# Reordering the rounds of attention on one core: maxima, scores, scores, maxima, and a unit's two projections side by side

## The reference, cut to what matters

```python
qk = x @ W_qk                        # 128 -> 2 * 16 * 64; values are the keys
q, k = jnp.split(qk, 2, axis=-1)     # 16 heads of 64
scores = einsum('bhid,bhjd->bhij', q * BETA, k)
scores = jnp.where(causal_mask, mask_value, scores)
attn = jax.nn.softmax(scores, axis=-1)
out = einsum('bhij,bhjd->bhid', attn, k)
return out.transpose(0, 2, 1, 3).reshape(b, n, 1024) @ W_out
```

## Time and profile before

| | before |
|---|---|
| median of 3 runs | 784.04 us (783.72 to 785.32) |
| the profiled execution | 783.28 us, of which 781.5 us from first to last instruction |
| busy: TensorE / VectorE / ScalarE / GpSimd | 729.7 / 458.5 / 375.6 / 424.4 us |
| mean granted clock of TensorE | 0.989 |

### The profile page before, as it was taken

One profiled execution on the slowest core, in us unless ns is written; L12 is line 12 of the kernel. 1 busy time (PEld: TensorE's weight loads), 2 busy tenths in 40 slices (PEclk: granted clock), 3 DMA queues, 4 the chain that ended last, 5 costly groups with the idle time before them and its releaser, 6 DMA issues. The chain is left out here.

```text
span 781.5 us, 14916 instructions
## 1 busy us (share of the span) xinstructions
PE 729.7 (93%) x5653; PEld 495.2 (63%) x5653; DVE 458.5 (59%) x1216; ACT 375.6 (48%) x476; POOL 424.4 (54%) x311
## 2 busy tenths in 40 slices
PE   2779999999999999999999998999989999789998
PEld 1456556555655655655655554887878875668887
DVE  5766665675676675576567540257565547766542
ACT  2355546545555545554654544235644534565421
POOL 4346865775684685676677567015455331344443
PEclk9699999999999999999999999999999999999999
DMA  2000010010010100101001001733222000033222
GB/s 67 7 7 20 19 32 16 22 28 15 22 28 16 25 23 22 25 18 29 15 15 28 16 23 33 177 81 97 76 89 95 29 1 0 3 118 108 91 95 81
DMA packets 41275, 33.47 MB, mean 43 GB/s; under 512 B 14002, under 2 KB 32756, under 8 KB 41204
## 3 DMA queue, kind: packets, MB, share of 16 engines
q1 hardware_dynamic: 41204, 32.52, 14.5%
HBM read 23.32 MB, written 1.31 MB: 32 GB/s over the span
## 5 line engine op out<-in xcount | busy, mean ns | idle before, releaser
L407 POOL TENSOR_TENSOR all_x<-all_x,at_probs 128x1024 f32<-128x1024 f32 (+3 forms) x128 | 215.3, 1682 | 31.8 <-ACT at_probs L487 17.1
L487 ACT ACTIVATE at_probs<-at_ring 128x1024 f32<-128x1024 f32 x144 | 147.5, 1026 | 123.0 <-PE at_ring L662 115.9
L532 DVE CUSTOM_DVE_ANT_0 at_ring<-at_ring,at_after_query 128x128 f32<-128x128 f32 (+3 forms) x256 | 119.5, 520 | 66.3 <-PE at_ring L627 66.3
L680 PE MATMUL at_out<-at_probs,at_k_nat 128*64 128x512 f32 (+3 forms) x768 | 140.3, 494 | 1.1 <-DVE a_attn_t L558 0.9
L407 POOL TENSOR_TENSOR all_x<-at_probs 128x768 f32<-128x768 f32 (+1 forms) x32 | 66.9, 2092 | 126.6 <-ACT at_probs L487 126.4
L1134 POOL TENSOR_TENSOR m_prod<-m_gate,m_wb 128x512 f32<-128x512 f32 x64 | 82.9, 1304 | 96.0 <-ACT m_gate L989 86.1
L680 PEld LDWEIGHTS at_out<-at_probs,at_k_nat 128*64 128x64 f32 x768 | 49.2, 136 | 70.0 <-issue 66.1
L528 DVE TENSOR_REDUCE at_half_max<-at_ring 128x2 f32<-128x1024 f32 x64 | 75.4, 1221 | 11.8 <-PE at_ring L627 11.8
L1043 DVE TENSOR_TENSOR m_hid<-m_prod,m_u 128x512 f32<-128x512 f32 x64 | 43.3, 685 | 66.5 <-POOL m_prod L1134 66.3
L653 PE MATMUL at_ring<-at_qh,at_kh 64*128 64x512 f32 (+3 forms) x384 | 73.8, 380 | 6.1 <-DVE at_m_rows L546 2.6
L909 PEld LDWEIGHTS m_acc<-rest_wd,m_hid 128*128 128x128 f32 x576 | 74.7, 191 | 6.0
(11 more groups left out here) (244 smaller groups left out, 1256.6 us busy)
## 6 DMA issues: line engine op xcount, KB each, us to landing
m_wb<-m_wt_far SPq DMA_DIRECT2D x128, 128.0 KB, 2.9
at_inv<-at_inv_q SPq DMA_DIRECT2D x240, 32.0 KB, 1.8
all_x<-in_L_attn_a_x SPq DMA_DIRECT2D x8, 256.0 KB, 3.7
at_w_raw<-in_L_attn_a_W_qk SPq DMA_DIRECT2D x8, 128.0 KB, 2.8
out<-all_x SPq DMA_DIRECT2D x4, 256.0 KB, 3.9
a_room<-in_L_attn_a_W_out SPq DMA_DIRECT2D x1, 512.0 KB, 4.1
m_raw_wg<-in_L_ffn_experts_wg SPq DMA_DIRECT2D x1, 512.0 KB, 4.2
m_raw_wu<-in_L_ffn_experts_wu SPq DMA_DIRECT2D x1, 512.0 KB, 4.1
```

Source lines behind the costliest of these rows:

```text
L407: return pool.tensor_tensor(sums[:, :, a * P:b * P], left, right, ALU.add)
L487: act.activation(probs[:, :, slot * BANK:(slot + 1) * BANK], pair("S", unit, slot)[:, :, :], ACT.Exp, scale=BETA).then_inc(exp_done, 1)
L532: last = dve.tensor_tensor_reduce(out=sums_ps, in0=sums_ps, in1=after_query[:, BANK - w:BANK], scale=1.0, scalar=MASKED, op0=ALU.add, op1= ...
L680: last = pe.matmul(out_ps[rows(l), o:o + (b - a) * P], k_nat[g % 3][:, j, rows(l)], probs[:, l, at:at + (b - a) * P], start=(j == 0), stop ...
```

## The change

- `ROUNDS` gets a new order. Each round has maxima at both ends and scores between them: M S M in round 0, M S S M in the others. M0 and M1 move from round 1 to round 0.
- The projection Q of a unit moves from round 0 of the unit before to the end of round 4 one unit earlier, directly behind K; for unit 1 it moves in front of the loop. Its copy on ScalarE and its subtraction on VectorE move with it.
- `keys_low` moves on VectorE from the end of round 4 to the end of round 0 of the next unit. Before the loop, queries_low(1) now stands ahead of keys_low(1).
- A new function `mask` issues the mask's matmuls for all diagonal tiles of a slot before its scores. They open the accumulation in the slot's banks, and the scores of such a slot add to them. For slots 1 and 7 the mask is issued ahead of the maxima that stand before the slot.

```diff
-ROUNDS = [[("S", 0)], [("S", 1), ("M", 0), ("S", 2), ("M", 1)], [("S", 3), ("M", 2), ("S", 4), ("M", 3), ("M", 4)],
-          [("S", 5), ("M", 5), ("S", 6), ("M", 6), ("M", 7)], [("M", 8), ("S", 7), ("M", 9), ("S", 8)]]
+ROUNDS = [[("M", 0), ("S", 0), ("M", 1)], [("mask", 1), ("M", 2), ("S", 1), ("S", 2), ("M", 3)],
+          [("M", 4), ("S", 3), ("S", 4), ("M", 5)], [("M", 6), ("S", 5), ("S", 6), ("M", 7)],
+          [("mask", 7), ("M", 8), ("S", 7), ("S", 8), ("M", 9)]]
+DIAGONAL = [slot for slot in range(NSLOT) if any(a == j for j, a, _ in SLOTS[slot])]
...
 # scalar queue
                 keys_high(1)
+                queries_high(1)
...
-                        if r == 0 and more:
-                            queries_high(unit + 1)
                         if r == NBURST - 1 and unit + 2 < UNITS:
                             keys_high(unit + 2)
+                            queries_high(unit + 2)
...
 # vector queue
                 join_maxima(0)
+                queries_low(1)
                 keys_low(dve, 1)
...
                             if unit:
                                 scale_out(unit - 1, 0)
-                            if more:
-                                queries_low(unit + 1)
                         for what, m in row:
                             if what == "M" and more:
                                 maxima(unit + 1, m)
+                        if r == 0 and unit and more:
+                            keys_low(dve, unit + 1)
...
                             if more:
                                 max_rows(unit + 1)
                             if unit + 2 < UNITS:
-                                keys_low(dve, unit + 2)
+                                queries_low(unit + 2)
...
 # tensor queue
+                def mask(unit, slot):
+                    if slot == 0:
+                        pe.wait_ge(rows_done, unit + 1)
+                    pair_free(pe, "S", unit, slot)
+                    diagonal = [(at_slot(slot, seg) - slot * BANK) for seg, (j, a, _) in enumerate(SLOTS[slot]) if a == j]
+                    for o in diagonal:
+                        for h in range(2):
+                            for l in range(2):
+                                pe.matmul(pair("S", unit, slot)[:, l, o:o + P], mask2[rows(l), h, :], eye2[rows(l), h, :],
+                                          start=(o == 0 and h == 0), stop=False, skip_group_check=True)
...
-                            pe.matmul(to[l], kh[u][rows(l), keys], qh[u][rows(l), q], start=True, stop=False)
+                            pe.matmul(to[l], kh[u][rows(l), keys], qh[u][rows(l), q], start=first, stop=False,
+                                      skip_group_check=True)
...
-                        for h in range(2 if a == j else 0):
-                            for l in range(2):
-                                pe.matmul(to[l][:, 0:P], mask2[rows(l), h, :], eye2[rows(l), h, :], start=False, stop=False)
...
                 project(1, "K")
+                project(1, "Q")
...
+                            if what == "mask":
+                                mask(unit, n)
+                            elif what == "S":
+                                if n in DIAGONAL and ("mask", n) not in row:
+                                    mask(unit, n)
                                 scores(unit, n)
...
-                        if r == 0 and more:
-                            project(unit + 1, "Q")
                         if r == NBURST - 1 and unit + 2 < UNITS:
                             project(unit + 2, "K")
+                            project(unit + 2, "Q")
```

More of the change, by code:

```diff
@@ L224, in ring_uses @@
 def ring_uses():
-    uses = [("K", 0, 0), ("Q", 0, 0), ("T", 0, 0)] + [("M", 0, m) for m in range(NMAX)] + [("K", 1, 0)]
+    uses = [("K", 0, 0), ("Q", 0, 0), ("T", 0, 0)] + [("M", 0, m) for m in range(NMAX)] + [("K", 1, 0), ("Q", 1, 0)]
     for unit in range(UNITS):
@@ L231, in ring_uses @@
                 uses.append(("T", unit + 1, 0))
-            uses += [(what, unit if what == "S" else unit + 1, n) for what, n in row if what == "S" or more]
-            if r == 0 and more:
-                uses.append(("Q", unit + 1, 0))
+            uses += [(what, unit if what == "S" else unit + 1, n) for what, n in row if what == "S" or what == "M" and more]
             if r == NBURST - 1 and unit + 2 < UNITS:
-                uses.append(("K", unit + 2, 0))
+                uses += [("K", unit + 2, 0), ("Q", unit + 2, 0)]
     return uses
@@ L638, in turn_max @@
                           .then_inc(rows_ps_ready, 1)
+                def mask(unit, slot):
[8 more added lines that the diff above has]
+                                          start=(o == 0 and h == 0), stop=False, skip_group_check=True)
                 def scores(unit, slot):
-                    u, out = unit % 2, pair("S", unit, slot)
+                    u, out, first = unit % 2, pair("S", unit, slot), slot not in DIAGONAL
                     if slot == 0:
@@ L652, in scores @@
                         for l in range(2):
-                            pe.matmul(to[l], kh[u][rows(l), keys], qh[u][rows(l), q], start=True, stop=False)
+                            pe.matmul(to[l], kh[u][rows(l), keys], qh[u][rows(l), q], start=first, stop=False,
+                                      skip_group_check=True)
                         for l in range(2):
-                            pe.matmul(to[l], kh[u][rows(l), keys], ql[u][rows(l), q], start=False, stop=False)
+                            pe.matmul(to[l], kh[u][rows(l), keys], ql[u][rows(l), q], start=False, stop=False,
+                                      skip_group_check=True)
                         for l in range(2):
-                            pe.matmul(to[l], kl[u][rows(l), keys], qh[u][rows(l), q], start=False, stop=False)
-                        for h in range(2 if a == j else 0):
-                            for l in range(2):
-                                pe.matmul(to[l][:, 0:P], mask2[rows(l), h, :], eye2[rows(l), h, :], start=False, stop=False)
+                            pe.matmul(to[l], kl[u][rows(l), keys], qh[u][rows(l), q], start=False, stop=False,
+                                      skip_group_check=True)
                         for l in range(2):
-                            last = pe.matmul(to[l], ones_r[rows(l), :], m_rows[u][rows(l), q], start=False, stop=True)
+                            last = pe.matmul(to[l], ones_r[rows(l), :], m_rows[u][rows(l), q], start=False, stop=True,
+                                             skip_group_check=True)
                             if seg + 1 == len(SLOTS[slot]):
@@ L729, in _ @@
                         for what, n in row:
-                            if what == "S":
+                            if what == "mask":
[3 more added lines that the diff above has]
+                                    mask(unit, n)
                                 scores(unit, n)
```

## The result

The changed kernel takes 762.39 us (median of 4 runs, 761.02 to 762.94) against 784.68 us before (4 runs, 783.72 to 786.04): ratio 0.971, 95% interval 0.969 to 0.974. The forecast was 763.6, inside 758 to 771.

The account below looks back on a forecast made before the run. TensorE was taken to set attention's length, with gain only from its standstills. Thirteen periods (-21.1), the start (+1.7) and the last full unit (-1.0) sum to -20.4 us, giving 763.6, range 758 to 771 (8 in 10).

Parts of the forecast that it names:

- Order of the rounds: Reordered maxima and scores in the rounds: all five TensorE stalls at the bank ring go, -1.36 us a period, at least -0.89.
- five standstills: TensorE waits at the ring of three bank pairs: 0.30, 0.17, 0.30, 0.16 and 0.43 us, 1.36 a period.
- Q beside K: Projection Q directly behind K at the end of round 4: 1.73 us instead of 2.02, -0.29 a period, bounds 0 to -0.39.
- Masks first: Masks issued before a slot's scores: same matmuls, taken as 0 a period, bounds 0 and -0.24.
- The chain of Q: Next unit's Q copy, max_rows, queries_low before the first mask of S0 at t = 3.33 after turn_max: cost 0, bounds 0 and +0.5.
- keys_low: Moved on VectorE behind round 0's maxima: cost 0; +2.6 us in all if it took its longest, 2.42 us.
- Period: One turn_max to the next in mid-attention: -1.62 us, from 28.21 to 26.6; thirteen of them give -21.1.
- The start: Queue before the loop delays unit 0's first scores: second turn_max at 66.0 instead of 64.31, +1.7 us, bounds +0.5 and +2.8.
- The last full unit: Unit without projections behind its last maxima, so turn_max waits: 25.6 us instead of 26.61, -1.0, bounds 0 and -2.8.
- more: Rival: doubled masks pay once (-3.1 us) and the start loses little (-1.2): 759.3 us, chance 0.12.
- part given back in round 0: Rival: S0 and M1 stall behind the copies in round 0, 0.5 us a period, +6.5: 770.1 us, chance 0.15.
- The slower one: Rival: K copy, Q copy and queries_low delay S0's mask, 2.15 us a period, +28: 791 us, chance 0.04.

Follow-up runs that it names:

- e1: Kernel before with only the projection Q moved beside K, old round order and masks: period 28.00 us, 781.03 us, ratio 0.996.
- e2: Changed kernel with the mask's matmuls back inside each segment, ahead of its last two matmuls: period 26.83 us, 768.69 us, ratio 0.979 to the kernel before.
- e3: Changed kernel with the last scores of round 4 (S8) again behind the last maxima (M9): period 26.91 us, 767.16 us, ratio 0.977 to the kernel before.
- e10: Changed kernel with masks of slots 1 and 7 directly ahead of their scores, behind the maxima, still grouped: period 26.71 us, 766.82 us, ratio 0.977.
- e5: Changed kernel with keys_low back at the end of round 4 on VectorE, in front of queries_low: period 27.30 us, 774.63 us, ratio 0.989.
- after_again: The changed kernel itself, unaltered, run again: period 26.48 us, 762.30 us, ratio 0.971 to the kernel before.
- e6: Changed kernel with M9 ahead of S8 in the last full unit (14) alone: period 26.48 us, 760.00 us, ratio 0.969 to the kernel before.
- e4: Changed kernel with the old order of maxima and scores in rounds 1 to 3: period 27.38 us, 776.77 us, ratio 0.989 to the kernel before.
- e7: Changed kernel with turn_max(0) between unit 1's K and Q, max_rows(0) ahead of queries_low(1), keys_low(1) behind unit 0's M1 maxima: 759.74 us, ratio 0.970.
- e9: e8 plus S0 ahead of M0 in round 0 and keys_low behind M2's maxima: period 26.48 us, 757.35 us, ratio 0.965 to the kernel before.
- e8: Changed kernel with the edits of e6 and e7 together: period 26.48 us, 758.61 us, ratio 0.967 to the kernel before.

## Why the prediction was right

The time was within 1.2 us and the mechanism the one given, but several terms were off and cancelled in part.

- *Order of the rounds*: -1.36 forecast, -1.18 measured (e1 to e2). All five standstills went, and e3 shows the one at S8 to be worth 0.43 as read. What came back is mostly at M1: not only the wait of 0.03 to 0.05 that I had put down, but 0.10 more on the step that had waited. I called the gap between M3 and S4 the shortest, at 2.27 us; it is not. Between M4 and M5, and M6 and M7, lie only two slots of 0.93, and there the slack is 0.40.
- *Q beside K*: -0.29 forecast, -0.20 measured (e1). I gave S0's last step its 0.23 back, but it still stands before 128-row work in e1 and stays at 0.42.
- *Masks first*: 0 forecast with a bound of 0.24; 0.35 measured. This bound failed. I had said that there is no pair of adjacent masks; there is, in the three slots with two diagonal tiles, whose second mask now stands behind the first, and I had put it down as worth 0.08 each at most. What I missed is the place: behind outputs the bf16 masks take up the 0.10 of the change of rows (e10, 0.23 of the 0.35).
- *The chain of Q* and *keys_low*: cost 0, as forecast. The mask starts at t = 3.36 (forecast 3.33), queries_low is done at 2.86 (2.95), and keys_low is 1.22 in all units. e5 shows what the lost slack costs: 0.82.
- *Period*: 26.6 forecast, 26.48 measured. The parts are -1.18, -0.20 and -0.35, -1.73 in all, where I had -1.36, -0.29 and 0.03, -1.62: the masks gave more than the two others lost, and that the sum comes so near is in part luck.
- *The start*: the second turn_max at 66.0 forecast, 66.12 measured (66.50 in after_again), by luck. Q ended earlier, because the clock rose within the projections (steps of 0.23 from 38.12 on), and S0 started at 44.02, not 44.7; but the wait of 3.04 in front of it was followed by the low clock until past 51 us, which I hadn't in the sum.
- *The last full unit*: 25.6 forecast, 25.30 measured. Its wait had a second price behind it, which the sum lacked: the granted clock. The stretch behind the last turn_max is 325.24 us, and 323.67 without the wait (e6), 1.57 less.

The rivals: none of them holds as a whole. Of *more*, the half with the masks came true (0.35 a period, 4.6 us, where it had 3.1) and the half with the start did not. Of *part given back in round 0*, only M1 lost time, 0.14 a period and not 0.5. The slower one's mechanism exists (e5), but it had 0.5 us to spare.

## What to carry to other kernels

Where the busy share says 93% and the waits say nothing, measure starts against starts: the standstills of 0.16 to 0.43 us, which modelled ends hide in whole or in part, were 15 of the 22 us that the 13 periods gained here. With a ring of n banks, write down for each use which one it waits for, and what lies between; two short users of different engines at either side of two long ones gave each release more than a slot's length. And look at the last iteration by itself: the order that is right in the middle left a wait there that cost 2.9 us in the traces with its clock (25.30 against 23.96, and 1.57 behind it), 2.4 us by the medians.

## What the runs showed of the hardware that I had not expected

- A bf16 group of four 128-column matmuls between fp32 ones costs TensorE 0.09 to 0.10 us and 0.08 on the step behind it. Behind work on all 128 rows it takes up the 0.10 that the change to 64 rows costs an fp32 matmul.
- A matmul that had to wait for a bank is itself about 0.1 longer until the next one starts (M7 in e4, 0.44 against 0.33; M1 in the changed kernel, 0.43).
- TensorE's clock fell behind the wait of 1.75 at the last turn_max in all seven traces that have this wait (the change, e2, e4, e5, e7, e10, after_again), and in none of the seven without it; it cost about 1.6 us. A standstill of the same length far behind attention, which all 14 traces have, lowered the clock in five of them (e1, e3, e4, e9, e10). In e9 and e8 TensorE waits 1.73 and 1.74 us for the same VectorE instruction; behind it e9 has the clock at 0.68 of full speed over 5 us, e8 at 1.00. The stretch behind the last turn_max is 325.25 us in e9 and 323.62 in e8. What decides it stays open.

TensorE's waits in e9 and in e8, then the stretch behind each:

```profile
654.60 0.83 PE L1002 MATMUL m_misc<-all_ident,m_w 128*16 128x128 f32 x4 [1.73 <-DVE m_w L1122]
```

```profile
655.51 0.60 PE L1002 MATMUL m_misc<-all_ident,m_w 128*16 128x128 f32 x4 [1.74 <-DVE m_w L1122]
```

```profile
655.00:660.00 5.00, 5.00 (x28) 4.80 (x26) 1.65 (x6) 1.48 (x3) 1.27 (x1) 0.68 0.15 39
```

```profile
656.00:661.00 5.00, 4.60 (x31) 3.32 (x29) 3.25 (x14) 3.17 (x5) 1.27 (x1) 1.00 0.18 62
```
